# Strided attention on one core: near maxima in four tiles of the array, and weightings in three groups instead of five

## The reference

```
xn = layernorm(x)
q, k, v = heads(xn @ q_w), heads(xn @ k_w), heads(xn @ v_w)
scores = (q * sigmoid(unity)) k^T / sqrt(16)
allowed = (key % 4 == 0) or (|query - key| <= 8)
attn = softmax(where(allowed, scores, -inf)) v
out = x + attn @ o_w + o_b + fp8(xn) @ w8^T + bias
```

## Time and profile before

| | |
|---|---|
| median of three runs | 1088.07 us (1084.07 to 1089.8) |
| the profiled execution | 1086.01 us, its span 1084.2 us |
| attention, first to last copy-out (L1012) | 229.86 to 1025.10 us |
| PE, DVE, ACT busy over the span | 95%, 86%, 77% |

### The profile page before, as it was taken

How to read it: one execution, slowest core, us unless ns; L and a number is a source line. 1 busy time by engine, 2 the same in 40 slices (tenths; PEclk the granted TensorE clock), 3 DMA queues, 4 the chain that set the end, 5 groups by cost and what they waited for, 6 DMA issues and landing times.

```text
span 1084.2 us, 27687 instructions
## 1 busy us (share of the span) xinstructions
PE 1028.3 (95%) x10694; PEld 462.7 (43%) x10695; DVE 933.8 (86%) x1162; ACT 839.8 (77%) x1590; POOL 251.2 (23%) x387
## 2 busy tenths in 40 slices
PE   4999999699999999999999999999999999999898
PEld 2666666233333333333333333333333333333487
DVE  6989897889999999999999999999999999999133
ACT  4667674288888888888888888888888888888600
POOL 2444453012212121221212122212121222212100
PEclk9999999599999999999999999999999999999999
DMA  6787878213223333333333333323343332231166
GB/s 197 227 254 252 262 250 274 54 46 88 85 83 90 98 85 93 102 91 99 97 96 109 98 99 95 104 84 108 91 113 88 105 91 82 86 85 58 48 236 239
DMA packets 166777, 134.07 MB, mean 124 GB/s; under 512 B 70492, under 2 KB 145884, under 8 KB 166636
## 3 DMA queue, kind: packets, MB, share of 16 engines
q1 hardware_dynamic: 163912, 128.06, 39.3%
q10 hardware_dynamic: 2736, 4.26, 1.2%
HBM read 71.13 MB, written 59.84 MB: 121 GB/s over the span
## 4 chain that ended last, share of the span: by engine, by line
PE 76%; DVE 12%; issue 7%; DMA 2%; ACT 2%; DVEq 0%; ACTq 0%
PE ps_attend L1228 17%; PE ps_attend L1145 12%; DVE peak_far L1087 10%; PE ps_attend L1186 10%; PE ps_project L621 7%; PE ps_attend L1235 6%; PE ps_attend L1308 5%; PE ps_attend L1156 4%; PE ps_project L679 4%; PE ps_attend L1197 3%; PE ps_project L594 3%; PE ps_attend L1163 3%; PE ps_attend L1204 2%; DMA sums<-out_rows 2%; PE ps_project L656 1%
## 5 line engine op out<-in xcount | busy, mean ns | idle before, releaser
L1087 DVE TENSOR_REDUCE peak_far<-ps_attend 128x2 f32<-128x1024 f32 x512 | 608.5, 1220 | 41.0 <-PE ps_attend L1186 30.8
L1028 ACT ACTIVATE probs<-ps_attend 128x512 f32<-128x512 f32 x1024 | 541.1, 597 | 49.5 <-PE ps_attend L1145 46.3
L1228 PE MATMUL ps_attend<-probs,v_op 128*17 128x512 f32 x2048 | 270.1, 600 | 0.5 <-issue 0.5
L1145 PE MATMUL ps_attend<-q_op,k_op 51*128 51x512 f16 x1024 | 252.1, 387 | 4.9 <-ACT probs L1028 3.3
L1186 PE MATMUL ps_attend<-k_op,q_op 48*128 48x512 f16 x1024 | 189.6, 388 | 26.1 <-DVE peak_far L1087 15.5
L1033 ACT ACTIVATE probs<-ps_attend 108x512 f32<-108x512 f32 x256 | 138.7, 594 | 34.6 <-PE ps_attend L1163 34.6
L1145 PEld LDWEIGHTS ps_attend<-q_op,k_op 51*128 51x128 f16 x1024 | 76.8, 93 | 193.9 <-ACT probs L1028 137.4
L894 POOL CAST negmax<-peak 128x16 bf16<-128x16 f32 x64 | 12.6, 196 | 609.6 <-DVE peak L1070 609.6
L1090 DVE TENSOR_REDUCE peak_near<-ps_attend 128x8 f32<-128x864 f32 x128 | 131.0, 1023 | 10.5 <-PE ps_attend L1204 10.4
L885 POOL TENSOR_TENSOR out_rows<-out_rows,share_rows 128x512 f32<-128x512 f32 x64 | 81.4, 1272 | 66.1 <-DMA share_rows<-shares_dram 64.0
L621 PE MATMUL ps_project<-xT_parts,w_parts 128*128 128x512 f16 x384 | 90.6, 387 | 2.1 <-DVE xT_parts L465 2.1
(11 more groups left out here) (91 smaller groups left out, 937.4 us busy)
## 6 DMA issues: line engine op xcount, KB each, us to landing
share_rows<-shares_dram SPq DMA_DIRECT2D x64, 256.0 KB
attn_dram<-out_rows SPq DMA_DIRECT2D x64, 256.0 KB, 5.5
q_dram<-qk_parts SPq DMA_DIRECT2D x48, 256.0 KB, 4.7
k_dram<-qk_parts SPq DMA_DIRECT2D x48, 256.0 KB, 2.7
q_op<-q_dram SPq DMA_DIRECT2D x128, 96.0 KB, 2.4
k_op<-k_dram SPq DMA_DIRECT2D x64, 144.0 KB, 3.1
v_dram<-v_sb SPq DMA_DIRECT2D x16, 544.0 KB, 3.0
base<-in_x SPq DMA_DIRECT2D x16, 512.0 KB, 4.7
```

The source lines that it names most:

```text
L1028: ins = nc.scalar.activation(probs[:, r, h], ps_s[st.bank(kind)], ACT.Exp, scale=undo)
L1087: ins = nc.vector.tensor_reduce(peak_far[:, :, p, tile], banks, AX_X, ALU.max)
L1145: nc.tensor.matmul(bank, k[half(f, KM), keys], q[half(f, KM), p], start=True, stop=True).then_inc(s_ready, 1)
L1228: ins = nc.tensor.matmul(ps_o[h * VW:h * VW + VR], v[:, r, h * VR:(h + 1) * VR], probs[:, r, h], start=(r == 0), stop=False)
```

## The change

The near maxima get one unit per step instead of two. Its banks hold 8 groups of 60 columns (2 pairs, 4 tiles) for queries in halves of 64 (`SUB`), and each matmul uses a quarter of the array: 64 rows by one of the two heads, 64 columns by one of the two halves of queries. For this the mask is relative to the half and the same everywhere (`near_q`, `near_k`, two new loads at the start), and the edges of the key rows are filled by four POOL copies of 48 x 6 values whenever a new group of heads begins (every fourth step; `set_edges`), in place of memsets. The far keys of the two pairs now lie beside each other in the key tile. The order of PE, `SCORE_PAIRS`, `MAXIMA` and the place of the copy-out are rewritten. Line numbers shift by about 20: far scores L1145 to L1168, far maxima L1186 to L1209, near scores L1156 and L1163 to L1179 and L1186, weightings L1228 and L1235 to L1248 and L1255, the small matmul L1136 to L1159.

```diff
-UNITS = TT * PAIRS + TT // 2
+UNITS = TT * PAIRS + 1
-AHEAD = 5
+AHEAD = 4
 SCORE_PAIRS = (
-    ("far", 0, 0), ("far", 0, 1), ("far", 2, 1), ("far", 1, 0), ("far", 1, 1),
-    ("near", 0), ("far", 2, 0), ("negmax",), ("far", 3, 1), ("far", 3, 0),
+    ("far", 0, 0), ("far", 0, 1), ("far", 2, 1), ("far", 1, 0), ("near", 0),
+    ("far", 1, 1), ("far", 2, 0), ("negmax",), ("far", 3, 1), ("far", 3, 0),
     ("near", 1),
 )
-COPY_AFTER = ("far", 1, 3)
+COPY_AFTER = ("far", 1, 1)
 MAXIMA = (
-    ("far", 2, 1), ("far", 1, 0), ("far", 0, 0), ("near", 0), ("far", 2, 0),
-    ("far", 3, 1), ("far", 1, 1), ("far", 3, 0), ("near", 1), ("far", 0, 1),
+    ("far", 2, 1), ("far", 1, 0), ("far", 0, 0), ("far", 2, 0),
+    ("far", 3, 1), ("far", 1, 1), ("near",), ("far", 3, 0), ("far", 0, 1),
 )
...
+        def set_edges(st):
+
+            k, it = k_op[st.parity(2)], st.iteration(2)
+            pool.wait_ge(k_loaded[st.parity(2)], 16 * 2 * 2 * PAIRS * (st.half_iteration(2) + 1))
+            edges = ((0, strided(0)), (SK - WPAD, strided(1)))
+            for i, (f, (to, of)) in enumerate(itertools.product(range(2), edges)):
+                nc.gpsimd.tensor_copy(k[half(f), to:to + WPAD], k[half(f), of:of + WPAD]).then_inc(edges_ready, 1)
+                pool.wait_ge(edges_ready, 4 * it + i + 1)
...
+            if st.queries(2) == 0:
+                pe.wait_ge(edges_ready, 4 * (st.iteration(2) + 1))
...
+            for sub, f in itertools.product(range(2), range(2)):
+                nc.tensor.matmul(banks[f][half(sub, SUB), 0:PAIRS * TT * NEAR], near_q[half(f)], near_k[half(f)],
+                                 start=True, stop=False)
+            for p, t in itertools.product(range(PAIRS), range(TT)):
+                for sub, f in itertools.product(range(2), range(2)):
+                    at = window(p, st.queries(2) * TT + t) + sub * SUB_STEP
+                    to = (p * TT + t) * NEAR
+                    ins = nc.tensor.matmul(banks[f][half(sub, SUB), to:to + NEAR],
+                                           q[half(f), p, t * P + sub * SUB:t * P + (sub + 1) * SUB],
+                                           k[half(f), at:at + NEAR], start=False,
+                                           stop=(p == PAIRS - 1 and t == TT - 1))
...
             far(2, 1)
+            far_unit(2, 0)
+            far(1, 0)
             weigh_last(3)
-            far(1, 0)
-            near_unit(0)
-            far_unit(2, 0)
-            far(1, 1)
             weigh_last(4)
             near(0)
             far_unit(3, 1)
+            far(1, 1)
             far_unit(1, 1)
             far(2, 0)
-            weigh_own(0)
             maxima()
+            near_unit()
             far(3, 1)
             far_unit(3, 0)
-            near_unit(1)
+            weigh_own(0)
+            weigh_own(1)
             far(3, 0)
-            weigh_own(1)
             near(1)
```

More of the change, by code:

```diff
@@ L65 @@
 BANDS = ((1, 18), (6, 6), (21, 5))
+SUB = HALF
+NEAR = (SUB + 2 * LOCAL) // STRIDE * (STRIDE - 1)
+SUB_STEP = SUB // STRIDE * (STRIDE - 1)
+NEAR_BANDS = ((1, 16), (4, 6), (12, 5))
 FP8_MAX = 448.0
@@ L80, in half, with strided, places @@
     return slice(f * HALF, f * HALF + n)
+def strided(u):
+    return WPAD + (S if u else S - NS)
+def places(u):
+    return WPAD + u * (S + NS)
 def load_k(eng, dram, k_op, loaded, it, pairs=tuple(itertools.product(range(2), range(PAIRS)))):
@@ L87, in load_k @@
         rows = dram["k"][it, u, f].rearrange("r i (c s) -> (r i) c s", c=CPB)
[L88 to L92, removed]
+        eng.dma_start(k_op[half(f), places(u):places(u) + S - NS].rearrange("r (c s) -> r c s", c=CPB),
+                      rows[:, :, ns:]).then_inc(loaded, 16)
+        eng.dma_start(k_op[half(f), strided(u):strided(u) + NS].rearrange("r (c s) -> r c s", c=CPB),
+                      rows[:, :, 0:ns]).then_inc(loaded, 16)
 def load_q(eng, dram, q_op, loaded, it, queries, slot):
@@ L287, in gpsimd_project @@
             nc.gpsimd.memset(zeros, 0.0).then_inc(zeros_set, 1)
-            for par in range(2):
-                nc.gpsimd.memset(keep["k_op"][par][:, 0:WPAD], 0.0).then_inc(pads_set, 1)
-                nc.gpsimd.memset(keep["k_op"][par][:, SK - WPAD:], 0.0).then_inc(pads_set, 1)
             nc.gpsimd.memset(keep["negmax"][:], 0.0).then_inc(pads_set, 1)
@@ L815, in part_attend @@
     k_loaded = keep["k_loaded"]
+    near_q, near_k = keep["near_q"], keep["near_k"]
+    edges_ready = sem("edges_ready")
     v_loaded = [sem(f"v_loaded{i}") for i in range(2)]
@@ L860, in window @@
     def window(p, tile):
-        return p * S + WSTEP * tile
-    def strided(p):
-        return WPAD + p * S + S - NS
+        return places(p) - WPAD + WSTEP * tile
     def close(tile):
@@ L869, in gpsimd_attend @@
     def gpsimd_attend(pool):
+        def set_edges(st):
[5 more added lines that the diff above has]
+                pool.wait_ge(edges_ready, 4 * it + i + 1)
+        pool.wait_ge(done["y8_ready"], B * CPB)
+        set_edges(Step(0, FIRST))
         pool.wait_ge(done["base_ready"], B * CPB)
-        pool.wait_ge(pads_set, 5)
+        pool.wait_ge(pads_set, 1)
         def add_bias(c):
@@ L901, in body @@
                                         ALU.subtract).then_inc(negmax_ready, 1)
+            if st.n >= 0 and st.exists(2) and st.queries(2) == 0:
+                pool.wait_ge(negmax_ready, st.at(2))
+                set_edges(st)
             if st.exists() and st.n % G == 1:
@@ L1069, in maximum @@
                     dve.wait_ge(negmax_ready, st.at())
[L1070 to L1071 removed]
+                nc.vector.tensor_tensor(peak[:, (st.n + 1) % 2], peak_far[:], peak_near[:], ALU.max
+                                        ).then_inc(peak_ready, 1)
             for i, kind in enumerate(MAXIMA):
@@ L1088, in body @@
                 else:
[L1089 to L1092, removed]
+                    ins = nc.vector.tensor_reduce(peak_near[:].rearrange("q f p t -> q f (p t)"),
+                                                  banks[:, :, 0:PAIRS * TT * NEAR].rearrange(
+                                                      "q f (g w) -> q f g w", w=NEAR), AX_X, ALU.max)
                 ins.then_inc(u_used, 2)
@@ new lines, in unit @@
+            for sub, f in itertools.product(range(2), range(2)):
[9 more added lines that the diff above has]
+                                           stop=(p == PAIRS - 1 and t == TT - 1))
+                    if p == PAIRS - 1 and t == TT - 1 and sub == 1:
+                        ins.then_inc(u_ready, 1)
@@ L1244, in far_unit, with near_unit @@
                 unit(st, ("far", tile, p))
-            def near_unit(tiles):
-                unit(st, ("near", tiles))
+            def near_unit():
+                unit(st, ("near",))
             def far(r, p):
@@ L1311, in project @@
             last.then_inc(y_ready, 1)
-        pe.wait_ge(keep["bands_loaded"], 16 * 6)
-        pe.wait_ge(pads_set, 5)
+        pe.wait_ge(keep["bands_loaded"], 16 * 8)
+        pe.wait_ge(pads_set, 1)
         pe.wait_ge(done["masks_ready"], 1)
@@ L1353, in build @@
             "k_op": [sb(f"k_op{i}", [P, SK], F16) for i in range(2)],
+            "near_q": sb("near_q", [P, SUB], BF16),
+            "near_k": sb("near_k", [P, PAIRS * TT * NEAR], BF16),
             "v_op": sb("v_op0", [P, NS // P + S // P, HG * VR]),
@@ L1416 @@
     near_k[:, :len(rows), :WPAD] = near_k[:, :len(rows), -WPAD:] = 1
+    at = np.arange(NEAR)
+    hot = np.concatenate([np.arange(n)[:, None] == at // size % n for size, n in NEAR_BANDS])
+    beside = np.abs(STRIDE * (at // 3) + 1 + at % 3 - LOCAL - np.arange(SUB)[:, None]) <= LOCAL
+    rel_k = np.zeros((2, HALF, PAIRS * TT, NEAR), np.float32)
+    rel_k[:, :len(hot)] = hot[:, None, :]
+    rel_q = np.zeros((2, HALF, SUB), np.float32)
+    rel_q[:, :len(hot)] = np.where(hot.astype(int) @ beside.T.astype(int), 0, -BIG)
     def bf16_bits(a):
@@ L1437 @@
         "minus": np.full((PARTS, SK), -PEAK_RANGE, np.float16),
+        "rel_q": bf16_bits(rel_q.reshape(P, SUB)),
+        "rel_k": bf16_bits(rel_k.reshape(P, PAIRS * TT * NEAR)),
     }
```

7 lines of the change are left out of this document (4 added, 3 removed).

## The result

The changed kernel took 1234.94 us in the median of four runs (1231.18 to 1236.77), the kernel before 1087.28 us beside it: a ratio of 1.1355, 95% interval 1.1314 to 1.1397. That is slower, on the side forecast, and 43 us beyond the forecast of 1192: inside the wide range of 1140 to 1250, outside the 1165 to 1215 that had a chance of 0.70.

What follows compares the result with a forecast made beforehand. The prediction took a closed loop of ACT and PE through three score banks as the bound: 1086.0 + 99.8 - 6.9 + 10.5 = 1189.4, 1192 on the median's scale; range 1165 to 1215 (chance 0.70), wide range 1140 to 1250.

Steps and rivals of the forecast that it cites:

- the longer step at full clock: Attention step with paired weightings: 14.19 against 12.58 us, 1.61 more, +99.8 us over 62 steps.
- the late sums: DVE's maxima held up while the reciprocal waits for its sums; taken as gone with the reciprocal a unit later, -6.9 us.
- quarters that do not overlap: Rival at the near unit: quarters run one after another, a unit of 1.5 to 3.3 us, 1223 to 1334; chance 0.12.
- The loop of ACT and PE sets the step: Attention step: a closed loop of ACT and PE through three score banks, 12.58 us; DVE fits beside it.
- The two waits: ACT idle 0.87 us before the copy-out and about 1.4 us before the first exponential of `far(3, 0)`.
- PE waits 0.04 us for the third of three close maxima: Maxima of `far_unit` 1,0; 0,0; 2,0, reduced 1.2 us apart: PE waits 0.04 us as the bank for `far(1, 0)` frees.
- The near unit, +10.5 us: New near unit on PE: 1.0 us, 0.83 hidden behind exponentials, 0.17 x 62 = +10.5 us; low end costs 0.
- PE waiting for ACT before `far(1, 1)` and `far(2, 0)`: Sign to look for in PE's order within a step; no size given and no term in the sum.
- That DVE sets the step of the kernel before: Rival: PE's order waits for DVE's maxima, so the step falls with DVE's 0.9 us, to 1021; chance 0.10.
- That one pair alone starves ACT: Rival: PE runs ahead at one of the two pairs of weightings, loop 13.3 us, 1137; chance 0.08.

Runs made afterwards that it cites:

- pair01: The kernel before with round 0 moved directly ahead of round 1, `far(3, 0)` and the second near unit behind both: 1165.50 us, ratio 1.0716.
- split01: The changed kernel with `far(3, 0)` moved between the weightings of rounds 0 and 1, opening that pair: 1150.73 us, ratio 1.0589.
- fill_same: The changed kernel with the matmuls of `far(1, 1)` and `far(2, 0)` issued twice into the same bank: 1193.35 us, ratio 1.0977.
- near_only: The changed kernel's near unit, edges and loads with the kernel before's order of scores, weightings and copy-out (no pairs): 1088.38 us, ratio 1.0017.

## Why the prediction was right in kind and short in size

The 146.6 us of the 62 steps add up as 62 x 1.77 = 109.7 for the longer step at full clock, 24 x 1.65 = 39.6 for the clock, 4.2 for the last step and two odd ones, and -7 for the late sums. The prediction had the first (as 99.8) and the last; that its wide range holds the result is luck, since its upper part was there for quarters that do not overlap, and the clock was in no term.

- *The loop of ACT and PE sets the step.* Right. 12.58 became 14.35 at full clock against 14.19 walked; pair01 came out at 13.72 against 13.74, split01 at 13.66 against 13.56. The two waits were foreseen at 0.87 and about 1.4 us and are 0.81 and 1.52.
- *PE waits 0.04 us for the third of three close maxima.* Mis-sized: the row shows PE waiting 0.57 us there, and ACT 0.16 in front of `far(1, 0)`, which is the whole difference of 14.35 and 14.19, 62 x 0.16 = 10 us. DVE was taken to be off the loop, and here it is on it.
- *The near unit, +10.5 us.* Mis-sized on the other side: 0.58 us, below the 0.83 that were free, so 0 in this order. I had taken 1.0 from the near weighting's 32 pairs; the unit's 32 pairs take a third of that time. The low end of 0.42, four quarters side by side, was the nearer one. These two errors cancel. The overhead of about 60 cycles a matmul that I weighed from the Trainium skill (TensorEngine Tiling (Array Packing), section Performance Considerations) is not borne out as a time for each matmul of the whole array: 0.36 us for 32 is 11 ns each. For each quarter by itself, the other reading that the prediction gave, it is not contradicted: eight in 0.36 us are 45 ns each.
- *The late sums go, -6.9 us.* Borne out: between 240 us and the last step DVE never waits for sums in the changed kernel, and the kernel before did nine times between 240 us and the 63rd copy, 8.7 us in all. Most of the 32 us of the earlier trace rows, 23.3, lie behind the 63rd copy and lengthen no step.
- *The price of PE's waits.* This is the step that failed, by leaving something out. "PE waiting for ACT before `far(1, 1)` and `far(2, 0)`" stood in the prediction as a sign to look for and had no term in the sum. It does have a price: in 24 of 62 steps the granted clock was at 1.2 GHz in the next pair, 1.65 us each, 40 us. (The last step is 3.6 us longer; fill_same, at 16.31, still has 2.0 of that, and its clock falls there too.) fill_same, where the clock holds in the other steps, takes 1193.35 us; the sum had 1191.5, so close only because the two errors above cancel.
- *Rivals.* That the quarters do not overlap fell with the unit's 0.58 us, where that rival began at 1.5. That DVE sets the step of the kernel before fell with near_only, where DVE has one reduction less and the step does not shrink. That one pair alone starves ACT fell with pair01 and split01: either costs about 0.7 to 1.1 us.

## What to carry to other kernels

Between two engines that hand over a few banks, it was here not the sum of work that counted but the longest stretch in which the first engine feeds nothing: lay release, load, the longest foreign piece of work and the feed end to end, and compare with what the banks hold. Putting like work together saved 0.11 us of switching (0.87 us from round to round in place of 0.98) and lengthened exactly that stretch; cutting it shorter paid, though it cost two more switches, until (as the rows suggest) DVE's maxima came next. And idle time of PE off the loop was not free: in 24 of 62 steps the clock was lower for the work that is on it.

## What was not expected of the hardware

- The clock fell although PE had been busy 2.95 of the 3.40 us before; 0.42 us more of PE's busy time in a step of 14.35 kept it at full speed in all steps but the last. What decides in which steps it falls was not settled.
- 32 load-and-matmul pairs of 60 columns through four quarters of the array took 0.36 us.
